# Nine tiles of an expert layer moved ahead of the last batch's routing, and a new order of work in the attention slots

## What is computed

```python
def attn(x, wq, wk, wv, wo):                       # 16 heads of 128
    q = rope(einsum('bim,mhd->bhid', x, wq))
    k = rope(einsum('bim,mhd->bhid', x, wk))
    v = einsum('bim,mhd->bhid', x, wv)
    s = einsum('bhid,bhjd->bhij', q, k) / 128      # causal mask
    return einsum('bhid,hdm->bim', softmax(s) @ v, wo)

def ffn(x):                                        # 16 experts, 4 for each token
    top_val, top_idx = top_k(x @ router_weight.T + router_bias, 4)
    scores = zeros.at[top_idx].set(softmax(top_val))
    gate, up = (x @ gate_up_proj + gate_up_proj_bias)[..., ::2], [..., 1::2]
    glu = min(gate, 7) * sigmoid(1.702 * min(gate, 7))
    out = ((clip(up, -7, 7) + 1) * glu) @ down_proj + down_proj_bias
    return (out * scores).sum(over experts)

x = x + layernorm(attn(layernorm(x)))
x = x + layernorm(ffn(layernorm(x)))
```

## Time and profile before

| | us |
|---|---|
| median of three runs | 540.48 |
| lowest and highest | 540.2, 541.03 |
| the profiled execution, its own time | 541.4 |
| its span in the trace | 539.6 |
| PE busy | 458.9 (85%) |
| DVE busy | 356.9 (66%) |
| ACT busy | 326.6 (61%) |
| POOL busy | 250.4 (46%) |

### The profile page before, as it was taken

One profiled execution on the slowest core, in us unless ns is written; L12 is line 12 of the kernel. 1 busy time (PEld: TensorE's weight loads), 2 busy tenths in 40 slices (PEclk: granted clock), 3 DMA queues, 4 the chain that ended last, 5 costly groups with the idle time before them and its releaser, 6 DMA issues.

```text
span 539.6 us, 11513 instructions
## 1 busy us (share of the span) xinstructions
PE 458.9 (85%) x3388; PEld 430.5 (80%) x3388; DVE 356.9 (66%) x1231; ACT 326.6 (61%) x810; POOL 250.4 (46%) x229
## 2 busy tenths in 40 slices
PE   2888889999999999999999998334999999999700
PEld 2787778899999999999999997324999999999600
DVE  3799777778676677766685854251776776766436
ACT  3677777677587677676767666132566565655402
POOL 1778675536222256344552253141355555555612
PEclk9999999999999999999999999755999999999955
DMA  7336652699800001001464567023366656655482
GB/s 228 103 118 204 204 178 87 205 371 368 282 2 21 1 13 44 23 24 56 142 213 143 154 213 224 1 83 109 52 101 104 98 94 102 105 88 91 52 235 94
DMA packets 63900, 67.86 MB, mean 126 GB/s; under 512 B 4640, under 2 KB 58720, under 8 KB 63840
## 3 DMA queue, kind: packets, MB, share of 16 engines
q1 hardware_dynamic: 54960, 55.79, 32.5%
q0 software_dynamic: 8304, 10.88, 12.2%
q10 hardware_dynamic: 576, 0.46, 0.3%
HBM read 32.63 MB, written 34.49 MB: 124 GB/s over the span
## 4 chain that ended last, share of the span: by engine, by line
PE 66%; DVE 16%; issue 6%; ACT 4%; DMA 3%; POOL 3%; SPq 1%; DVEq 0%; POOLq 0%; ACTq 0%
PE bank L1087 25%; PE bank L1313 16%; PE bank L1325 7%; PE bank L1146 4%; PE bank L1128 4%; DVE qkT L818 3%; PE bank L1136 2%; DVE by_cos L809 2%; PE bank L1300 2%; PE bank L1127 2%; PE bank L1148 2%; DVE stats L789 1%; ACT by_sin L565 1%; POOL rows_d L458 1%; DVE oT_l L843 1%
## 5 line engine op out<-in xcount | busy, mean ns | idle before, releaser
L455 POOL TENSOR_TENSOR by_sin<-by_sin,rope_sin 128x512 f32<-128x512 f32 x64 | 83.0, 1297 | 150.9 <-ACT by_sin L565 150.9
L555 POOL DMA_INDIRECT sum_d<-y,xg x47 | 73.1, 1555 | 74.7 <-ACT y L753 74.4
L1313 PE MATMUL bank<-xgT,gu_now 128*128 128x128 f32 x752 | 93.3, 278 | 0.4 <-DVE gu_now L1024 0.4
L565 ACT ACTIVATE by_sin<-bank 64x512 f32<-64x512 f32 x128 | 75.8, 592 | 24.2 <-DVE by_cos L809 22.7
L1313 PEld LDWEIGHTS bank<-xgT,gu_now 128*128 128x128 f32 x752 | 89.4, 195 | 0.7 <-DVE gu_now L1024 0.7
L1087 PE MATMUL bank<-xT_h,qk_h 128*128 128x256 f32 x256 | 78.6, 307 | 3.5 <-POOL qk_l L440 2.0
L1087 PE MATMUL bank<-xT_h,qk_l 128*128 128x256 f32 x256 | 73.5, 287 | 0.0
L1087 PE MATMUL bank<-xT_l,qk_h 128*128 128x256 f32 x256 | 73.2, 286 | 0.0
L587 ACT ACTIVATE prob<-score,row_bias 128x128 f32<-128x128 f32 (+1 forms) x128 | 56.9, 447 | 22.4 <-DVE row_bias L828 22.1
L843 DVE TENSOR_TENSOR oT_l<-bank,oT_h 128x256 fp32r<-128x256 f32 x64 | 27.1, 423 | 59.2 <-ACT oT_h L565 56.8
L818 DVE TENSOR_TENSOR qkT<-by_cos,by_sin 128x512 f32<-128x512 f32 x64 | 55.6, 869 | 1.1 <-POOL by_sin L455 1.1
(11 more groups left out here) (140 smaller groups left out, 1131.8 us busy)
## 6 DMA issues: line engine op xcount, KB each, us to landing
rows_d<-blank SPq DMA_DIRECT2D x32, 576.0 KB, 7.2
gu_w<-_L_ffn_gate_up_proj_dram SPq DMA_DIRECT2D x16, 512.0 KB
xg<-rows_d SPq DMA_DIRECT2D x47, 144.0 KB
dn_w<-in_L_ffn_down_proj_dram SPq DMA_DIRECT2D x16, 256.0 KB
sum_d<-blank SPq DMA_DIRECT2D x2, 1152.0 KB, 9.8
raw_qk<-in_L_attn_wq_dram SPq DMA_DIRECT2D x16, 128.0 KB, 3.5
raw_qk<-in_L_attn_wk_dram SPq DMA_DIRECT2D x16, 128.0 KB, 3.7
raw_v<-in_L_attn_wv_dram SPq DMA_DIRECT2D x8, 256.0 KB, 2.8
```

Source lines behind the costliest of these rows:

```text
L455: pool.tensor_tensor(v, v, rope_sin[:, :].unsqueeze(1).broadcast_to([P, 2, T]), ALU.mult).then_inc(pool_sin, 1)
L555: pool.indirect_dma_start(out=sum_d[i % SUMS], out_offset=bass.IndirectOffsetOnAxis(ap=xg[:, i % XG, TOKEN:TOKEN + 1].bitcast(U32), axis=0 ...
L565: return sc.activation(out, in_, ACT.Copy)
L1313: m = pe.matmul(ps_gu[i % 2][:, (2 * s + r) * P:(2 * s + r + 1) * P], gu_now[:, i % 2, k, s, r * P:(r + 1) * P], xgT[:, i % XT, k, :], sta ...
```

## The change

It has these parts.

- **Nine early tiles** (`EARLY = 9`). By the end of the third batch each expert's rows are known for 768 tokens, so the tiles that are full by then need nothing of the last batch; there are at least nine. DVE counts and plans them in slots 8 to 10 and 13 of the last batch (`count_early`, `plan_early`, `leave_out_early`, `early_table_out`) into `early_table`; the later plan leaves them out. SP fetches their rows once the scatters of three batches have landed and the buffers that share memory with them are free. After slot 63 each engine's order for the nine tiles and the last batch's steps is written out. Tiles 9 to 46 go through the loop.
- **Tables of ACT** for gelu and exp are loaded by small activations of their own (`load_table`).
- **Slot order.** `swap` waits for the products alone, `cosine` follows it and works in the PSUM bank, `rotate` adds the bank and `by_sin` at the end of the same slot; queries and keys of head n now wait for the rotation of head n-2, since it holds the bank. ACT and DVE have new orders in a slot, and some routing steps stand one to three slots later.
- **Start.** DVE zeroes a tile and PE multiplies it four times (`keep_busy`) before the inputs are there.
- Memory and PSUM banks are laid out anew for it, and `shift_x` moves behind the tile loop.

DVE's order in one plain slot, before and then after. `score` is filled by the row minimum, `oT_l` is the low part of the output, `by_cos` and `bank` hold the cosine product, `qkT` the rotated head, `prob` the probabilities.

The diff, cut to what the prediction speaks of:

```diff
+EARLY = ((N - T) * TOP - E * (P - 1) + P - 1) // P
...
             start_sum(2)
-            start_sum(3)
...
+            sp.wait_ge(dve_early_table, 1)
+            sp.wait_ge(dma_scatter, 16 * (TILES - 2) * TOP)
+            sp.wait_ge(pe_v, SLOTS // 2)
+            sp.wait_ge(pool_sin, SLOTS)
+            sp.wait_ge(dve_rope, SLOTS)
+            sp.wait_ge(pe_s, SLOTS)
+            for i in range(3):
+                load_rows(i)
+            load_dn(H // 2 - 1)
+            load_dn(E - 1)
+            for i in range(3, EARLY):
+                load_rows(i)
+            start_sum(3)
+            sp.wait_ge(dve_table, 1)
+            sp.wait_ge(dma_scatter, 16 * TILES * TOP)
+            for i in range(EARLY, TILE_MAX):
+                load_rows(i)
...
             def swap(n):
-                sc.wait_ge(dve_cos, n + 1)
+                sc.wait_ge(pe_qk, n + 1)
...
+                if n % 2 == 0 and n:
+                    values(n // 2)
                 if n + LEAD < SLOTS:
                     swap(n + LEAD)
+                probT_out(n)
                 if b == 0:
+                    if h + 6 < H:
+                        high_qk(h + 6)
+                    if h % 2 == 0 and h // 2 + 2 < H // 2:
                         high_v(h // 2 + 2)
...
+                if n + 2 < SLOTS:
+                    softmax_exp(n + 2)
+                if n + 3 == SLOTS:
+                    load_table(ACT.Gelu_apprx_sigmoid, 0)
+                if n == SLOTS - 1:
+                    sc.wait_ge(dve_early_table, 1)
+                    sc.wait_ge(dma_gu, 16 * E)
+                    xgT_out(0)
+                    experts = {0: place_gu(0)}
+                oT_high(n)
...
             def cosine(n):
-                dve.wait_ge(pe_qk, n + 1)
-                if n >= 2:
-                    dve.wait_ge(dve_rope, n - 1)
-                v = by_cos[:, n % 2, :].rearrange("p (b t) -> p b t", b=2)
...
+                dve.wait_ge(act_swap, n + 1)
+                v = ps_qk[n % 2][:, :].rearrange("p (b t) -> p b t", b=2)
+                dve.tensor_tensor(v, v, rope_cos[:, :].unsqueeze(1).broadcast_to([P, 2, T]), ALU.mult).then_inc(dve_cos, 1)
...
+            dve.memset(qkT[:, 0, :, :], 0.0).then_inc(dve_idle, 1)
...
                 if n >= 2:
-                    pe.wait_ge(act_swap, n - 1)
+                    pe.wait_ge(dve_rope, n - 1)
...
+            pe.wait_ge(dve_idle, 1)
+            keep_busy(qkT[:, 0, 0, 0:P], qkT[:, 0, :, :].rearrange("p w t -> p (w t)"), 4)
```

More of the change, by code:

```diff
@@ L542, in _, with add_rows @@
                         scatter(5, h - 9)
[L543 to L551 removed]
+            def add_rows(i):
                 pool.wait_ge(act_y, i + 1)
@@ L1054, in _ @@
             dve.wait_ge(dma_gu, 16 * E)
             experts = {0: place_gu(0)}
-            for i in range(TILE_MAX):
+            oT_low(SLOTS - 1)
+            experts[1] = place_gu(1)
+            clamp(0, experts[0])
+            experts[2] = place_gu(2)
+            attn_stats(B - 1)
+            clamp(1, experts[1])
+            experts[3] = place_gu(3)
+            residual(B - 1)
+            gated(0)
+            gated(1)
+            clamp(2, experts[2])
+            experts[4] = place_gu(4)
@@ new lines, in _ @@
+            gated(2)
+            clamp(3, experts[3])
+            choose(B - 1)
+            gated(3)
+            share(B - 1)
+            place(B - 1)
+            experts[5] = place_gu(5)
+            clamp(4, experts[4])
+            gated(4)
+            experts[6] = place_gu(6)
+            plan_tiles()
+            clamp(5, experts[5])
+            gated(5)
+            experts[7] = place_gu(7)
+            clamp(6, experts[6])
+            gated(6)
+            experts[8] = place_gu(8)
@@ L1057, in _ @@
+            table_out()
+            clamp(7, experts[7])
+            gated(7)
+            clamp(8, experts[8])
+            gated(8)
+            dve.wait_ge(dve_table, 1)
+            experts[EARLY] = place_gu(EARLY)
+            for i in range(EARLY, TILE_MAX):
                 if i + 1 < TILE_MAX:
@@ L1335, in _ @@
+            for i in range(EARLY, TILE_MAX + 2):
                 if i + 1 < TILE_MAX:
```

555 lines of the change are left out of this document (342 added, 213 removed).

## The result

The changed kernel takes 520.13 us (median of four runs, 517.41 to 520.65), the kernel before, beside it, 540.75 us (540.2 to 541.16). The ratio is 0.961, 95% interval 0.957 to 0.965: 3.9% faster. 516 was forecast, and 520 lies in the range from 507 to 528. The profiled execution took 519.65 us, its span is 517.8, the mean granted clock 0.965.

The account below looks back on a forecast made before the run. PE was taken as full in later slots and the tile loop, leaving gains in the first batch and hole. Start 2.9, first batch 6.0, later batches 0, hole 15.5: 541.4 - 24.4 = 517.0, less 0.9: 516 us; range 507 to 528.

Parts of the forecast that it names:

- The cheap sum: First batch: the rotation's sum reading one input from PSUM takes 0.69 us, bounds 0.68 and 1.38.
- the loop through `raw_v`: First batch: the single buffer, reloaded and cast at even heads, makes a loop of 10.3 us for two slots, 5.1 each.
- Rival (c): First batch gains nothing, since POOL holds the scalings and casts instead: 522 us; chance 0.10.
- rival (d): First batch runs at PE's floor of 4.6 us per slot: 509 us; chance 0.09.
- The new loop: Batches 1 to 3: the later oT copy closes a loop of 4.1 us, fitting PE's 4.50; effect 0.
- rival (a): Batches 1 to 3: slots bound by the new loop, deciding from 5.01 us; at 5.1, 545 us; chance 0.05.
- the case without cover: Last batch: the early plan's small DVE steps, if not hidden in DVE's free time, would cost 4 us.
- Step (1): Hole, from slot 60 to the statistics: they start at 20.3 us, 5.1 later than before.
- Step (2): Hole, statistics to slot numbers: 16.7 us instead of 14.1, so slot numbers at 37.0 us after slot 60.
- Step (3): Hole, slot numbers to tile 9's products: POOL's adds barely hidden, start of sums released at 52.4, products at 57.6 us.
- Rival (b): Hole filled but less shortened: PE drops to its lower clock, six tiles cost 9.6 us, 526 us; chance 0.14.
- Rival (e): Hole: early tiles don't run early because rows or expert weights arrive after it; 532 us; chance 0.04.

Follow-up runs that it names:

- `tiles_late`: Changed kernel with the nine early tiles and their early plan undone, new slots and start kept: 531.84 us (0.983 of the kernel before).
- `load_at_62`: Changed kernel with the first table load, for gelu, moved one slot later, ahead of the copy of oT 62 instead of oT 61: 523.12 us.
- `no_exp_load`: Changed kernel without the two table loads around the exponentials of the last batch's shares, a copy in place of these exponentials: 530.43 us.
- `after_again`: The changed kernel, unaltered, timed once more in a later group of runs: 523.13 us.
- `no_warm`: Changed kernel without the four products of the zeroed tile on PE at the start: 526.65 us.
- `no_warm_again`: The same changed kernel without the four products at the start, timed once more: 521.25 us.

## Why the prediction held, and where it was off

**The cheap sum.** Right: 692 ns beside POOL, for which 690 was taken.

**Slots of the first batch.** 4.93 us each, forecast 5.12, so 8.5 us less instead of 6.0. The term that was too large is the loop through `raw_v`, taken as 10.3 us for two slots with a load of some 3.2 us. Two slots take 9.9. The load took 2.7 us in the middle of eight, which is about the difference, and ACT did wait for it, four times and 2.1 us in all; that the loop alone sets the pace is not shown. Rival (c) falls by the same rows; rival (d), the floor of 4.6, was not reached.

**Start.** 2.5 and 1.0 in the two profiles, forecast 2.9 with bounds 0 and 4. Of the 1.5 us between the two, 0.5 stands before the first product already (10.07 and 10.53 us); the rest goes with the fall of the clock behind the warm-up.

**The new loop in batches 1 to 3.** Right that it fits: a plain slot of 4.50 us stays at 4.49 ((102.39 - 88.92) / 3), batches 1 and 2 are equal to 0.3 us, and rival (a) falls. Wrong that the early plan is hidden. It costs 1.3 us, by `tiles_late`, a third of the 4 us that were named for the case without cover. The cover was to be the 1.2 us a slot that DVE has free; that other late steps of the last batch use it too is likely, but not shown. Of the remaining 0.8 us of the 2.1, 0.6 are lost in the last batch as well (57.90 against 57.33 in `tiles_late`, cause open) and 0.2 in batches 1 and 2; all within the bounds of -3 and +5.

**The hole.** Forecast 57.6 us from slot 60 to tile 9's products, measured 59.9. Step (1), the statistics: 20.3 forecast, 21.0 measured; oT 61 was held by the table load, PE waited for it and its clock fell, and `load_at_62` takes 1.3 us back (19.7). Step (2), the slot numbers: 37.0 forecast, 35.9 measured, so 14.9 us from the statistics for a sum of 16.7; the wait for `expo` was sized at 1.5 and is 0.8 by `no_exp_load`. Step (3): the third add ended just ahead of the scatters, as forecast, and the start of the sums was released 1.3 us later than forecast (53.7 against 52.4; `started` ends at 370.53). Since the slot numbers were 1.1 early, this stretch, 15.4 us in the forecast, took 17.8: the 2.4 us are the largest miss in the hole. The clock was down over its first part, from 352.0 to 355.4; how much of the 2.4 us this costs, and how the rest divides over the tiles' handovers, is open. From the release to tile 9's products I had 5.2 us, and it took 6.1. Here the step that failed is that I followed tile 9's rows alone. Tile 9's copies were done at 375.43 (374.70 + 0.73), but PE turns tile 10 ahead of tile 9's products, and SyncE's eight requests take 8.79 us, 1.10 each; so PE waited 1.78 us for tile 10's rows, until 376.18, and some 1 us of that counts. Then the 16 products ran at the lower clock, 3.22 us for 2.02; the three falls cover 10.2 us in all, and the sum had none.

**Rival (b), the clock.** It happened in part. The clock fell three times for 3.4 us (from 328.1, 352.0 and 375.9), not over six tiles, and the mean from 340 to 360 is 0.91; in `after_again` the third fall lasted 6.8 us. Rival (e) falls by tile 0's products, 17.3 us after slot 60.

The total is 2.6 us of forecast gain missing: 2.3 in the hole, 2.1 in the slots, 0.4 at the start and 0.3 at the end, less 2.5 of a first batch that gained more. The errors of the first batch and of the later slots nearly cancel, so the total is closer than its terms, and that is luck. The median is off by more, 520.13 for 516: I took it 0.9 below the profiled execution, and here it lies 0.5 above.

## What to carry to other kernels

Where POOL and DVE both work on SBUF, put one of DVE's two inputs into PSUM; in this kernel that halved the operation and was worth some 8 us, but only with an order in which the engine that reads the bank first comes early in the slot. When a chain is followed to a tile, follow each engine's whole list there, and the next tile's steps that stand ahead in it as well. And before a difference of 1% between versions is explained, run the unaltered kernel again beside them.

## What the runs showed of the hardware

**A standstill that belongs to the run.** In `no_warm` PE has no work from 360.8 to 366.9, ACT none until 366.3 and DVE none from 363.1, while POOL's scatters go on, one in 1.27 us. ACT waits for nothing but PE's turning of tile 6, which is recorded long before. It stands at the same place in six kernels of two groups, on two chips, and in none of the other five profiles with early tiles, two of which come from a chip that had shown it. What separates the groups I can't say. One thing goes with it: in the profiles with the standstill about one semaphore record in seven is missing (5813 are there in `no_warm`, 6787 in `no_warm_again`). The Trainium skill (NOTIFIC — the notification-queue block, Interfaces) says that a filled internal queue of the block that writes these records can stall an engine. That would fit, but no run here tests it, and missing records don't make a standstill by themselves: `tiles_late`, timed beside `no_warm`, has as few (5799) and shows none. The kernel before shows no trace of the groups either: its medians in the five groups of runs lie from 540.75 to 541.53.

**A table load cost its own time alone here.** 1.28 us, with 0.02 us ahead of it and the next activation 0.01 us behind it.

**A short wait of PE can cost its clock.** PE waited 2.1 us for oT 61 until 327.54, and the granted clock was down from 328.1 to 331.5. It need not: three of nine profiles with this wait show no fall before 350. What a fall costs: the 16 products of tile 9 took 3.22 us in one, those of tile 0 2.02 us at the full clock.
